# A fused group-norm and 4-bit grouped convolution: a new prologue, a new statistics chain and end, and one store for two images

## The chip, the cores and the metric

The kernel runs on one core of a Trainium2 chip. The time is the device time of one execution in microseconds (us). Before the change it is 264.53 us, the median of 3 runs (264.43 to 264.54).

## What is computed

`x` has 32 images of 512 channels and 28x28 pixels in float32. Each image is normalised over 32 groups of 16 channels, giving `v`. Cut to what matters:

```python
v   = (x - mean_group) / sqrt(var_group + 1e-5)
xa  = round(clip((v[next conv group] - lA) / (uA - lA), 0, 1) * 15) / 15
wq  = 2 * (round(clip((weight - lW) / (uW - lW), 0, 1) * 15) / 15 - 0.5)
y   = einsum('bgihw,goi->bgohw', xa, wq.reshape(4, 128, 128))
y   = relu(batch_norm(y, gamma, beta, running_mean, running_var))
out = x + y + v
```

The kernel writes `max(conv, floor) + (x * y_scale + y_bias)`, where `floor` and the batch norm's offset are folded into per-channel constants. Input and output are 51.4 MB each.

## The kernel before

**Tiling.** 128 channels lie on the partitions, so an image is four tiles of 128x784, one per convolution group g; output group o of g is (g + 3) mod 4. `images` is a ring of 12 images in SBUF. An image is loaded into its place, read by every stage, turned in place into the output, and stored from there. Statistics and coefficients are made for a pair of images (u = n // 2), so that 16 chains serve 32 images.

**The steps of one image.** (1) Statistics: VectorE takes groups 0 and 1 (groups 0 to 2 for the first six images) with `bn_stats` (L435, `half_stats`), and at the pair's second image `sum_stats` (L443); ScalarE takes the other groups with a sum (L218) and a sum of squares (L224). (2) The chain of the pair: TensorE averages the means over norm groups (`average_means`, L533, L534, L536), ScalarE copies them (`copy_mean`, L232), GpSimd makes deviations (`deviations`, L350 to L357), TensorE averages their squares (`average_deviations`, L542), ScalarE takes the root (`deviation`, L238, L239), VectorE its reciprocal (`rough_rstd`, L468), and GpSimd a Newton step and the four coefficients (`coefficients`, L370 to L379, nine small instructions). (3) Quantise: three tiles on ScalarE (L251), one on GpSimd (L397), then VectorE caps all four at once into bf16 (`cap`, L450). (4) TensorE multiplies each tile by the weights in three bf16 parts (`multiply`, L552, 6 matmuls a tile, three PSUM sets, so tile k waits for `finish` of tile k - 3). (5) GpSimd scales and shifts the image in place (`affine`, L388), and VectorE adds the two (`finish`, L458).

**Order.** Every engine has an order written out by hand, in slots. In slot n VectorE does finish(n, 0), finish(n, 1), cap(n + 1), finish(n, 2), a half statistic, finish(n, 3), and three half statistics of image n + 6 (`AHEAD`); in odd slots `rough_rstd` stands before finish(n, 3). GpSimd does the four `affine` of image n + 1 and the tile of `quantise(n + 2)`, with `deviations` in even slots and `coefficients` at the end of odd ones. In a pair of slots ScalarE does statistics of image n + 6 with `copy_mean` inside, six quantises, `deviation`, and statistics of image n + 7. TensorE puts `average_means` ahead of multiply(n + 1, 0) in even slots and `average_deviations` ahead of multiply(n + 1, 3).

**DMA.** SyncE loads (L183); from image 12 on, the load of image n waits for the store of image n - 12. ScalarE stores images 0 to 27 one by one (L244), each behind a wait for that image's last `finish`; it does so at two places of its pair of slots. SyncE stores images 28 to 30 (L187) and image 31 in four pieces (L196).

**Prologue.** Image 0 is loaded in four pieces, then the weights, then images 1 to 11. GpSimd quantises the weights (L336 to L341) before it turns to the first deviations; the four limits reach all 128 partitions through a broadcast DMA (L204).

Of the kernel before, what the change touches and what calls it, by code (L numbers as in the profile page):

```python
# [5 lines left out]
ALU = mybir.AluOpType  # L6
ACT = mybir.ActivationFunctionType
AXIS = mybir.AxisListType
F32 = mybir.dt.float32
# [12 lines left out]
AHEAD = 6  # L22
ACT_STORES = 28
# [5 lines left out]
def fused_norm_quantised_conv(nc, x, weight, limits, channel_params, out):  # L29
# [14 lines left out]
    def stats_on_dve(u):  # L44
        return 3 if u < AHEAD // 2 else 2


    def quant_on_act(n):
        return 2 if n == 0 else 3

# [18 lines left out]
    with ExitStack() as ctx:  # L69
# [20 lines left out]
        half_var = sb("half_var", [P, 2, G], F32)  # L90
        std = sb("std", [P, 2, G], F32)
        rough = sb("rough", [P, 2, G], F32)
        newt = sb("newt", [P, 3, 2, G], F32)
        three_halves = sb("three_halves", [P, 2, G], F32)
        minus_half = sb("minus_half", [P, G], F32)
        rstd = sb("rstd", [P, 2, G], F32)
        mean_rstd = sb("mean_rstd", [P, 2, G], F32)
        q_scale = sb("q_scale", [P, 2, 2, G], F32)
        q_bias = sb("q_bias", [P, 2, 2, G], F32)
        y_scale = sb("y_scale", [P, 2, 2, G], F32)  # L100
        y_bias = sb("y_bias", [P, 2, 2, G], F32)
# [6 lines left out]
        cols = sb("cols", [P, 4, G], F32)  # L108
        bounds = sb("bounds", [P, 4], F32)
        w_rng = sb("w_rng", [P, 2], F32)  # L110
        a_rng = sb("a_rng", [P, 5], F32)
        bn = sb("bn", [P, 5, G], F32)
        bias_bn = sb("bias_bn", [P, G], F32)
# [14 lines left out]
        first_loaded = [sem(f"first_loaded{g}") for g in range(G)]  # L128
        x_loaded = [sem(f"x_loaded{j}") for j in range(RING)]
        stored = [sem(f"stored{j}") for j in range(RING)]  # L130
# [31 lines left out]
        y_ready = sem("y_ready")  # L162
# [4 lines left out]
        def wait_image(engine, n, g):  # L167
            if n == 0:
                engine.wait_ge(first_loaded[g], DMA)
            else:  # L170
                engine.wait_ge(x_loaded[n % RING], DMA * (n // RING + (1 if n % RING else 0)))

        @block.sync
        def _(sync):
            for g in (0, G - 1, 1, 2):
                sync.dma_start(images[:, 0, g], x_v[0][:, g]).then_inc(first_loaded[g], DMA)
            sync.dma_start(w_raw[:], weight.rearrange("(g o) i -> o g i", o=P)).then_inc(weights_in, DMA)

            def load(n):
                j = n % RING  # L180
                if n >= RING:
                    sync.wait_ge(stored[j], DMA * (n // RING))
                sync.dma_start(images[:, j], x_v[n]).then_inc(x_loaded[j], DMA)  # L183
# [5 lines left out]
            for n in range(1, B):  # L189
                load(n)  # L190
            for n in range(ACT_STORES, B - 1):
                store(n)
            for g in range(G):
                o = output_group(g)
                sync.wait_ge(final, G * (B - 1) + g + 1)
                sync.dma_start(out_v[B - 1][:, o], images[:, (B - 1) % RING, o]).then_inc(stored[(B - 1) % RING], DMA)  # L196
            for j in range(RING):
                stores = len(range(j, B, RING)) + (G - 1 if j == (B - 1) % RING else 0)
                sync.wait_ge(stored[j], DMA * stores)

        @block.scalar
        def _(act):
            act.dma_start(rows[:], channel_params.rearrange("k (g p) -> (k g) p", p=P)).then_inc(rows_in, DMA)
            act.dma_start(bounds[:], limits.to_broadcast([P, 4])).then_inc(limits_in, DMA)  # L204
# [3 lines left out]
            nc.scalar.activation(cols[:], cols_ps[:, 0:4 * G], ACT.Identity).then_inc(cols_done, 1)  # L208
# [32 lines left out]
            def store(n):  # L241
                if 0 <= n < ACT_STORES:
                    act.wait_ge(final, G * n + G)
                    act.dma_start(out_v[n], images[:, n % RING]).then_inc(stored[n % RING], DMA)  # L244

            def quantise(n, g):
                u, j = n // 2, n % 2
                act.wait_ge(coef_done, u + 1)
                if n >= 2:
                    act.wait_ge(capped, n - 1)  # L250
                nc.scalar.activation(levels[:, n % 2, g], images[:, n % RING, g], ACT.Relu,  # L251
                                     bias=q_bias[:, u % 2, j, g:g + 1],
                                     scale=q_scale[:, u % 2, j, g:g + 1]).then_inc(q_act, 1)
# [15 lines left out]
            copy_mean(1)  # L269
            image_stats(4)  # L270
            deviation(1)
            for g in range(quant_on_act(1)):
                quantise(1, g)
            image_stats(5)

            for n in range(0, B - 2, 2):
                u, m = n // 2 + 2, n + AHEAD
                if m < B:
                    take_sum(m, 2)
                    take_sum(m, 3)  # L280
# [12 lines left out]
                store(n)  # L293
                if m + 1 < B:
                    image_stats(m + 1)

            for n in range(B - 3, ACT_STORES):
                store(n)

        @block.gpsimd  # L300
        def _(pool):
# [9 lines left out]
            nc.gpsimd.memset(three_halves[:], 1.5)  # L311
            nc.gpsimd.memset(minus_half[:], -0.5)
# [19 lines left out]
            nc.gpsimd.tensor_tensor(bias_bn[:], cols[:, 1], bn[:, 4], ALU.subtract)  # L332

            pool.wait_ge(ranges_done, 1)
            pool.wait_ge(weights_in, DMA)
# [267 lines left out]
```

## Time and profile before

| | |
|---|---|
| median of 3 runs | 264.53 us |
| the profiled execution: its time, its span | 266.27 us, 264.5 us |
| busy share of the span: VectorE, GpSimd, ScalarE, TensorE | 89%, 89%, 77%, 70% |
| bytes moved, mean rate | 103.28 MB, 390 GB/s |
| share of the chain that ended last on GpSimd | 72% |

The span is that of one profiled execution on the core; the time of that execution has some 1.8 us around it. A busy share is an average over the prologue, 26 like slots, and an end without loads and statistics. The rate of the DMA engines is the second resource that everything shares.

### The profile page before, as it was taken

What the parts mean: (1) busy time and instruction counts of PE and PEld (TensorE: products, weight loads), DVE (VectorE), ACT (ScalarE), POOL (GpSimd) and SP (SyncE); (2) the same over time, 40 slices, a digit from 0 to 9 for tenths busy, and PEclk for the clock granted to TensorE, in tenths of its full rate; (3) what the DMA queues carried; (4) which work ended last, traced back from release to release, by engine and by line L of the source; (5) the groups of instructions that cost most, each with busy time, mean ns of one, the idle gap of its engine ahead of it and who ended that gap; (6) DMA issues with size and microseconds to landing.
All of it is one profiled execution on the core that took longest, in us unless ns stands there. A gap on an engine that the chain in (4) does not pass through costs nothing.

```text
span 264.5 us, 4055 instructions
## 1 busy us (share of the span) xinstructions
PE 184.9 (70%) x997; PEld 103.7 (39%) x997; DVE 235.7 (89%) x359; ACT 204.7 (77%) x378; POOL 235.4 (89%) x383
## 2 busy tenths in 40 slices
PE   0024498677779797788868678978777797775870
PEld 0023455344445453444425244445443454432330
DVE  1476989999999999999999999999999999795790
ACT  2344699999898999899998989898989696908000
POOL 6395689999999999999999999999999999999940
PEclk9999999999979899988999997979999869999597
DMA  5999999999999999999999999999999999999468
GB/s 154 402 410 410 410 406 408 414 397 331 417 416 416 408 417 417 415 417 417 414 413 417 416 417 417 415 415 417 415 417 417 417 412 402 393 397 375 178 243 327
DMA packets 34614, 103.28 MB, mean 390 GB/s; under 512 B 1296, under 2 KB 1824, under 8 KB 34592
## 3 DMA queue, kind: packets, MB, share of 16 engines
q1 hardware_dynamic: 19632, 58.07, 55.7%
q10 hardware_dynamic: 14960, 44.97, 42.6%
q8 instruction: 8, 0.13, 0.2%
q14 instruction: 14, 0.11, 0.1%
HBM read 51.65 MB, written 51.38 MB: 389 GB/s over the span
## 4 chain that ended last, share of the span: by engine, by line
POOL 72%; issue 9%; DVE 5%; PE 5%; DMA 3%; ACT 2%; ACTq 1%; POOLq 1%; DVEq 0%; SPq 0%
POOL images L388 50%; POOL levels L397 7%; DMA images<-in_x 3%; PE prod L552 2%; POOL q_bias L378 2%; DVE stats L435 2%; PE var_ps L542 1%; ACT levels L251 1%; POOL newt L371 1%; DVE images L458 1%; POOL newt L372 1%; POOL rstd L373 1%; POOL dev L350 1%; POOL mean_rstd L374 1%; POOL dev L353 1%
## 5 line engine op out<-in xcount | busy, mean ns | idle before, releaser
L552 PE MATMUL prod<-codes,w_t 128*128 128x392 bf16 x768 | 156.2, 354 | 35.2 <-DVE images L458 21.0
L388 POOL TENSOR_SCALAR images<-images,y_scale,y_bias 128x784 f32<-128x784 f32 x128 | 147.7, 1167 | 0.0
L458 DVE SCALAR_TENSOR_TENSOR images<-prod,floor,images 128x784 f32<-128x784 f32 x128 | 126.9, 1016 | 3.0 <-PE prod L552 2.0
L552 PEld LDWEIGHTS prod<-codes,w_t 128*128 128x128 bf16 x768 | 73.7, 105 | 109.2 <-issue 54.6
L251 ACT ACTIVATE levels<-images,q_bias,q_scale 128x784 int16<-128x784 f32 x95 | 90.3, 1029 | 9.5 <-POOL y_bias L379 9.1
L435 DVE BATCH_NORM_STATS2 stats<-images 128x6 f32<-128x392 f32 x140 | 70.7, 551 | 11.0 <-DMA images<-in_x 11.0
L218 ACT ACTIVATE unused<-images 128x784 bf16<-128x784 f32 x58 | 49.2, 851 | 11.8 <-DMA images<-in_x 10.9
L224 ACT ACTIVATE unused<-images,sums 128x784 bf16<-128x784 f32 x58 | 54.6, 944 | 3.0 <-issue 2.8
L450 DVE TENSOR_SCALAR codes<-levels 128x3136 bf16<-128x3136 int16 x32 | 42.2, 1319 | 4.3 <-POOL levels L397 4.2
L397 POOL TENSOR_SCALAR levels<-images,q_scale,q_bias 128x784 int16<-128x784 f32 x33 | 32.9, 998 | 0.1
L542 PE MATMUL var_ps<-dev,avg 128*128 128x8 f32 x128 | 18.5, 271 | 13.6 <-POOL dev L357 13.6
L542 PEld LDWEIGHTS var_ps<-dev,avg 128*128 128x128 f32 x128 | 17.2, 208 | 18.9 <-POOL dev L357 18.8
L533 PE MATMUL mean_ps<-sums,avg 128*128 128x4 f32 (+1 forms) x32 | 5.3, 235 | 19.2 <-DVE sums L443 19.2
L533 PEld LDWEIGHTS mean_ps<-sums,avg 128*128 128x128 f32 x32 | 6.3, 214 | 20.8 <-DVE sums L443 19.8
L224 ACT ACTIVATION_READ_ACCUMULATOR unused<-images,sums 128x1 f32 x58 | 11.2, 193 | 0.0
L218 ACT ACTIVATION_READ_ACCUMULATOR unused<-images 128x1 f32 x58 | 11.2, 192 | 0.0
L232 ACT ACTIVATE gmean<-mean_ps 128x8 f32<-128x8 f32 x16 | 2.8, 174 | 10.5 <-PE mean_ps L534 10.5
L536 PE MATMUL var_ps<-sums,avg_n 128*128 128x8 f32 x32 | 6.5, 276 | 0.0
L534 PE MATMUL mean_ps<-sums,avg_one 128*128 128x4 f32 (+1 forms) x32 | 6.4, 271 | 0.0
L238 ACT ACTIVATE half_var<-var_ps,eps 128x8 f32<-128x8 f32 x16 | 4.0, 253 | 3.0 <-PE var_ps L542 3.0
L370 POOL TENSOR_TENSOR newt<-rough 128x8 f32<-128x8 f32 x16 | 3.2, 201 | 3.5 <-DVE rough L468 3.5
L336 POOL TENSOR_SCALAR w_rest<-w_raw,bounds,w_rng 128x512 f32<-128x512 f32 x1 | 2.1, 2087 | 4.4 <-DVE a_rng L478 4.4
(60 smaller groups left out, 84.9 us busy)
## 6 DMA issues: line engine op xcount, KB each, us to landing
images<-in_x SPq DMA_DIRECT2D x31, 1568.0 KB, 13.2
out<-images ACTq DMA_DIRECT2D x28, 1568.0 KB, 15.5
out<-images SPq DMA_DIRECT2D x3, 1568.0 KB, 5.5
images<-in_x SPq DMA_DIRECT2D x4, 392.0 KB, 6.1
out<-images SPq DMA_DIRECT2D x4, 392.0 KB, 5.5
w_raw<-in_weight SPq DMA_DIRECT2D x1, 256.0 KB, 7.6
rows<-in_channel_params ACTq DMA_DIRECT2D x1, 8.0 KB, 2.3
bounds<-in_limits ACTq DMA_DIRECT2D x1, 2.0 KB, 6.2
```

What stands on the lines that cost most here:

```text
L218: nc.scalar.activation(unused[:, g % 2], images[:, n % RING, g], ACT.Identity, scale=1.0 / HW, accum_out=sums[:, u % 2, 0, j, g:g + 1]).th ...
L224: nc.scalar.activation(unused[:, g % 2], images[:, n % RING, g], ACT.Square, scale=-1.0, bias=sums[:, u % 2, 0, j, g:g + 1], accum_out=sum ...
L251: nc.scalar.activation(levels[:, n % 2, g], images[:, n % RING, g], ACT.Relu, bias=q_bias[:, u % 2, j, g:g + 1], scale=q_scale[:, u % 2, j ...
L388: nc.gpsimd.tensor_scalar(here, here, y_scale[:, u % 2, j, o:o + 1], y_bias[:, u % 2, j, o:o + 1], ALU.mult, ALU.add).then_inc(y_ready, 1)
L397: nc.gpsimd.tensor_scalar(levels[:, n % 2, g], images[:, n % RING, g], q_scale[:, u % 2, j, g:g + 1], q_bias[:, u % 2, j, g:g + 1], ALU.mu ...
L435: nc.vector.bn_stats(two, images[:, n % RING, g, h * HALF:(h + 1) * HALF]).then_inc(bn_done, 1)
L450: nc.vector.tensor_scalar(codes[:, n % 2], levels[:, n % 2], 0.0, TOP, ALU.max, ALU.min).then_inc(capped, 1)
L458: nc.vector.scalar_tensor_tensor(out=two, in0=prod[:, k % SETS, :, 0:HALF], scalar=floor[:, o:o + 1], in1=two, op0=ALU.max, op1=ALU.add).t ...
L533: nc.tensor.matmul(mean[:, :, 0:k], avg[:], sums[:, par, 0, :, 0:k], start=True, stop=True)
L536: nc.tensor.matmul(var_ps[:, 0:2 * G], avg_n[:], sums[:, par, 1], start=True, stop=False)
L542: done = nc.tensor.matmul(var, avg[:], dev2[:, :, :, s], start=False, stop=(s == SUBSETS - 1))
L552: done = nc.tensor.matmul(prod[:, k % SETS, h, 0:HALF], w_t[:, part, output_group(g)], codes[:, n % 2, g, h * HALF:(h + 1) * HALF], start= ...
```

## The change

- **Prologue.** Images 0 and 1 are loaded in four pieces each. VectorE, not GpSimd, quantises the weights. The limits come as one row of 16 bytes, and TensorE spreads them with a one-row matmul into `cols`. TensorE turns the weights before the first averages. Multiply(0, 0) goes ahead of the means of pair 1.
- **Chain.** `AHEAD` is 5, and VectorE takes three groups for the first four images only. `average_means`, `copy_mean` (behind the first of three quantises), `deviations` (behind the second affine) and `deviation` (behind an image's statistics) all stand in an odd slot; `rough_rstd` stands behind finish(n, 0) and `coefficients` behind affine(n + 1, 0) of the next, even slot. `coefficients` has seven instructions, of which the last two make all four coefficients.
- **End.** For the last four images ScalarE does two of the four `affine`.
- **Stores.** ScalarE issues one DMA for two images in even slots, behind that slot's statistics and ahead of its quantises, for images 0 to 29. There is one `stored` semaphore per pair of ring places, so a load of image 12 or later waits for the store of both. SyncE stores image 30, and image 31 in four pieces.

```diff
-AHEAD = 6
-ACT_STORES = 28
+AHEAD = 5
+SINGLE = 2
+HELPED = 4
+ACT_STORES = 30
 SETS = 3
...
-        return 3 if u < AHEAD // 2 else 2
+        return 3 if u < 2 else 2
 
 
     def quant_on_act(n):
         return 2 if n == 0 else 3
+
+
+    def affine_on_act(n):
+        return 2 if n >= B - HELPED else 0
+
...
-            for g in (0, G - 1, 1, 2):
-                sync.dma_start(images[:, 0, g], x_v[0][:, g]).then_inc(first_loaded[g], DMA)
-            sync.dma_start(w_raw[:], weight.rearrange("(g o) i -> o g i", o=P)).then_inc(weights_in, DMA)
+            for n in range(SINGLE):
+                for g in (0, G - 1, 1, 2):
+                    sync.dma_start(images[:, n, g], x_v[n][:, g]).then_inc(first_loaded[n][g], DMA)
+                if n == 0:
+                    sync.dma_start(w_raw[:], weight.rearrange("(g o) i -> o g i", o=P)).then_inc(weights_in, DMA)
 
             def load(n):
                 j = n % RING
                 if n >= RING:
-                    sync.wait_ge(stored[j], DMA * (n // RING))
+                    sync.wait_ge(stored[j // 2], DMA * (n // RING))
                 sync.dma_start(images[:, j], x_v[n]).then_inc(x_loaded[j], DMA)
 
             def store(n):
                 sync.wait_ge(final, G * n + G)
-                sync.dma_start(out_v[n], images[:, n % RING]).then_inc(stored[n % RING], DMA)
...
+                sync.dma_start(out_v[n], images[:, n % RING]).then_inc(stored[n % RING // 2], DMA)
+
+            for n in range(SINGLE, B):
                 load(n)
...
-            act.dma_start(bounds[:], limits.to_broadcast([P, 4])).then_inc(limits_in, DMA)
+            act.dma_start(limit_row[:], limits).then_inc(limits_in, DMA)
...
-                if 0 <= n < ACT_STORES:
-                    act.wait_ge(final, G * n + G)
-                    act.dma_start(out_v[n], images[:, n % RING]).then_inc(stored[n % RING], DMA)
+            def store_pair(u):
+                act.wait_ge(final, 2 * G * (u + 1))
+                k = u % (RING // 2)
+                act.dma_start(out_v[2 * u:2 * u + 2].rearrange("j p g f -> p j g f"),
+                              images[:, 2 * k:2 * k + 2]).then_inc(stored[k], DMA)
...
+            def affine(n, g):
+                u, j, o = n // 2, n % 2, output_group(g)
+                act.wait_ge(q_act, q_act_until(n - 1) + o + 1)
+                here = images[:, n % RING, o]
+                nc.scalar.activation(here, here, ACT.Identity, bias=coef[:, u % 2, 1, 1, G * j + o:G * j + o + 1],
+                                     scale=coef[:, u % 2, 0, 1, G * j + o:G * j + o + 1]).then_inc(y_act, 1)
...
-            copy_mean(1)
-            image_stats(4)
-            deviation(1)
-            for g in range(quant_on_act(1)):
-                quantise(1, g)
-            image_stats(5)
-
-            for n in range(0, B - 2, 2):
-                u, m = n // 2 + 2, n + AHEAD
-                if m < B:
-                    take_sum(m, 2)
-                    take_sum(m, 3)
-                    take_squares(m, 2)
-                if u < PAIRS:
-                    copy_mean(u)
-                store(n - 1)
-                if m < B:
-                    take_squares(m, 3)
-                for g in range(quant_on_act(n + 2)):
-                    quantise(n + 2, g)
-                for g in range(quant_on_act(n + 3)):
-                    quantise(n + 3, g)
-                if u < PAIRS:
-                    deviation(u)
-                store(n)
-                if m + 1 < B:
-                    image_stats(m + 1)
-
-            for n in range(B - 3, ACT_STORES):
-                store(n)
+
+            for n in range(-1, B - 1):
+                m = n + AHEAD
+                if n % 2:
+                    u = (n + 3) // 2
+                    for g in range(quant_on_act(n + 2) if n + 2 < B else 0):
+                        quantise(n + 2, g)
+                        if g == 0 and u < PAIRS:
+                            copy_mean(u)
+                    if m < B:
+                        image_stats(m)
+                    if u < PAIRS:
+                        deviation(u)
+                    for g in range(G - affine_on_act(n + 1), G):
+                        affine(n + 1, g)
+                else:
+                    for g in range(G - affine_on_act(n + 1), G):
+                        affine(n + 1, g)
+                    if m < B:
+                        image_stats(m)
+                    if n:
+                        store_pair(n // 2 - 1)
+                    for g in range(quant_on_act(n + 2) if n + 2 < B else 0):
+                        quantise(n + 2, g)
...
-            pool.wait_ge(ranges_done, 1)
-            pool.wait_ge(weights_in, DMA)
-            chained(nc.gpsimd.tensor_scalar(w_rest[:], w_raw[:], bounds[:, 0:1], w_rng[:, 1:2], ALU.subtract, ALU.mult))
...
-            for g in range(G):
-                scaled = nc.gpsimd.tensor_scalar(w_raw[:, g], w_rest[:, g], bn[:, 3, g:g + 1], None, ALU.mult)
-            scaled.then_inc(w_scaled, 1)
...
-                linked(u, 4, nc.gpsimd.tensor_tensor(rstd[:], newt[:, 2], rough[:], ALU.mult))
-                nc.gpsimd.tensor_tensor(mean_rstd[:], gmean[:, par], rstd[:], ALU.mult).then_inc(coef_step, 1)
-                nc.gpsimd.tensor_scalar(q_scale[:, par], rstd[:], a_rng[:, 2:3], None, ALU.mult)
-                nc.gpsimd.tensor_scalar(y_scale[:, par], rstd[:], 1.0, None, ALU.add)
-                pool.wait_ge(coef_step, LINKS * u + 5)
-                nc.gpsimd.tensor_scalar(q_bias[:, par], mean_rstd[:], a_rng[:, 4:5], a_rng[:, 3:4], ALU.mult, ALU.add)
-                nc.gpsimd.tensor_tensor(y_bias[:, par], bias_bn[:].unsqueeze(1).to_broadcast([P, 2, G]), mean_rstd[:],
-                                        ALU.subtract).then_inc(coef_done, 1)
+                linked(u, 4, nc.gpsimd.tensor_tensor(norm[:, 0], newt[:, 2], rough_, ALU.mult))
+                linked(u, 5, nc.gpsimd.tensor_tensor(norm[:, 1], gmean[:, par].rearrange("p j g -> p (j g)"), norm[:, 0],
+                                                     ALU.mult))
+                linked(u, 6, nc.gpsimd.tensor_tensor(scaled[:], norm[:].unsqueeze(2).to_broadcast([P, 2, 2, 2 * G]),
+                                                     coef_mul[:].unsqueeze(3).to_broadcast([P, 2, 2, 2 * G]), ALU.mult))
+                nc.gpsimd.tensor_tensor(coef[:, par], scaled[:], coef_add[:], ALU.add).then_inc(coef_done, 1)
...
             coefficients(0)
             quantise(0)
-            deviations(1)
-            affine(0, 0)
-            affine(0, 1)
-            coefficients(1)
-            affine(0, 2)
-            affine(0, 3)
-            quantise(1)
-            for n in range(B - 1):
-                for g in range(G):
+            for n in range(-1, B - 1):
+                mine = G - affine_on_act(n + 1)
+                for g in range(mine):
                     affine(n + 1, g)
-                if n % 2 == 0 and n // 2 + 2 < PAIRS:
-                    deviations(n // 2 + 2)
+                    if n % 2 and g == 1 and (n + 3) // 2 < PAIRS:
+                        deviations((n + 3) // 2)
+                    if n % 2 == 0 and g == 0 and (n + 2) // 2 < PAIRS:
+                        coefficients((n + 2) // 2)
                 if n + 2 < B:
                     quantise(n + 2)
-                if n % 2 == 1 and (n + 3) // 2 < PAIRS:
-                    coefficients((n + 3) // 2)
...
+            group_stats(0, 0)
+            dve.wait_ge(cols_done, 1)
...
+            group_stats(0, 1)
+            group_stats(0, 2)
+
+            dve.wait_ge(weights_in, DMA)
+            chained(nc.vector.tensor_scalar(w_rest[:], w_raw[:], bounds[:, 0:1], w_rng[:, 1:2], ALU.subtract, ALU.mult))
...
+            dve.wait_ge(floor_done, 1)
+            for g in range(G):
+                done = nc.vector.tensor_scalar(w_raw[:, g], w_rest[:, g], bn[:, 3, g:g + 1], None, ALU.mult)
+            done.then_inc(w_scaled, 1)
 
             image_stats(1)
             sum_stats(0)
-            image_stats(2)
-            rough_rstd(0)
-
             dve.wait_ge(w_turned, 1)
...
+            group_stats(2, 0)
+            group_stats(2, 1)
+            rough_rstd(0)
+            group_stats(2, 2)
             image_stats(3)
             sum_stats(1)
             cap(0)
             image_stats(4)
-            rough_rstd(1)
-            image_stats(5)
-            sum_stats(2)
-            dve.wait_ge(floor_done, 1)
 
             for n in range(B):
                 m = n + AHEAD
                 finish(n, 0)
+                if n % 2 == 0 and (n + 2) // 2 < PAIRS:
+                    rough_rstd((n + 2) // 2)
                 finish(n, 1)
                 if n + 1 < B:
                     cap(n + 1)
                 finish(n, 2)
                 if m < B:
                     half_stats(m, 0, 0)
-                if n % 2 == 1 and (n + 3) // 2 < PAIRS:
-                    rough_rstd((n + 3) // 2)
                 finish(n, 3)
                 if m < B:
...
+            pe.wait_ge(limits_in, DMA)
+            nc.tensor.matmul(cols_ps[:, 4 * G:5 * G], one_row[:], limit_row[:], start=True,
+                             stop=True).then_inc(cols_turned, 1)
...
-            average_means(0)
-            average_deviations(0)
             pe.wait_ge(w_scaled, 1)
-            pe.wait_ge(cols_done, 1)
             for g in range(G):
                 turned = nc.tensor.transpose(prep_ps[:, g], w_raw[:, g], ident[:])
             turned.then_inc(w_turned, 1)
-            average_means(1)
-            average_deviations(1)
+            average_means(0)
+            average_deviations(0)
             pe.wait_ge(w_ready, 1)
-            for g in range(G):
-                multiply(0, g)
-
-            for n in range(B - 1):
-                chain = n % 2 == 0 and n // 2 + 2 < PAIRS
+
+            for n in range(-1, B - 1):
+                chain = n % 2 == 1 and (n + 3) // 2 < PAIRS
+                if chain and n > 0:
+                    average_means((n + 3) // 2)
+                multiply(n + 1, 0)
+                if chain and n < 0:
+                    average_means((n + 3) // 2)
                 if chain:
-                    average_means(n // 2 + 2)
-                multiply(n + 1, 0)
+                    average_deviations((n + 3) // 2)
                 multiply(n + 1, 1)
                 multiply(n + 1, 2)
-                if chain:
-                    average_deviations(n // 2 + 2)
                 multiply(n + 1, 3)
```

## Rows read from the trace of the kernel before

**Rows 1.** The page: busy time and share by engine; the DMA's total.
```profile
PE 184.9 (70%) x997; PEld 103.7 (39%) x997; DVE 235.7 (89%) x359; ACT 204.7 (77%) x378; POOL 235.4 (89%) x383
...
DMA packets 34614, 103.28 MB, mean 390 GB/s; under 512 B 1296, under 2 KB 1824, under 8 KB 34592
```

**Rows 2.** The chain that ended last, two pieces: start us, us, engine, tile, line, count.
```profile
181.73 4.63 POOL images L388 x4
...
195.93 4.64 POOL images L388 x4
```

**Rows 3.** Stretches: us, busy time by engine, granted clock, DMA share, GB/s.
```profile
54.50:66.50 12.00, 9.13 (x54) 4.75 (x53) 11.97 (x20) 11.65 (x23) 11.77 (x16) 1.00 1.00 360
70.00:200.00 130.00, 103.20 (x571) 56.30 (x570) 129.69 (x194) 122.63 (x230) 126.48 (x201) 0.93 1.03 416
...
225.00:240.00 15.00, 12.23 (x74) 6.65 (x74) 12.31 (x14) 6.91 (x10) 14.61 (x23) 1.00 1.01 393
```

**Rows 4.** ScalarE's first store, by line and in its stretch: issue and landing.
```profile
L244 ACTq DMA_DIRECT2D out<-images x1: 402/402/402, 46.1 to 46.1; - x1
...
DMA to landing us min/median/max: 11.9/11.9/11.9
```

**Rows 5.** Timeline, VectorE: start us, us, engine, line, operation, count, idle time before.
```profile
202.33 1.70 DVE L450 TENSOR_SCALAR codes<-levels 128x3136 bf16<-128x3136 int16 x1
...
208.06 1.97 DVE L458 SCALAR_TENSOR_TENSOR images<-prod,floor,images 128x784 f32<-128x784 f32 x2
209.94 1.01 DVE L450 TENSOR_SCALAR codes<-levels 128x3136 bf16<-128x3136 int16 x1
...
214.64 1.01 DVE L458 SCALAR_TENSOR_TENSOR images<-prod,floor,images 128x784 f32<-128x784 f32 x1
```

**Rows 6.** Timeline, from finish(26, 0) to the copy of the means.
```profile
222.26 1.96 DVE L458 SCALAR_TENSOR_TENSOR images<-prod,floor,images 128x784 f32<-128x784 f32 x2
...
223.43 1.16 PE L552 MATMUL prod<-codes,w_t 128*128 128x392 bf16 x6 [1.34 <-DVE images L458]
...
224.96 0.18 ACT L232 ACTIVATE gmean<-mean_ps 128x8 f32<-128x8 f32 x1 [2.19 <-PE mean_ps L534]
```

**Rows 7.** Timeline, ScalarE: two statistics in a row, six quantises, the root.
```profile
48.32 0.85 ACT L218 ACTIVATE unused<-images 128x784 bf16<-128x784 f32 x1
...
52.05 0.86 ACT L218 ACTIVATE unused<-images 128x784 bf16<-128x784 f32 x1
...
213.23 5.69 ACT L251 ACTIVATE levels<-images,q_bias,q_scale 128x784 int16<-128x784 f32 x6
...
218.82 0.25 ACT L238 ACTIVATE half_var<-var_ps,eps 128x8 f32<-128x8 f32 x1
218.97 0.25 ACT L239 ACTIVATE std<-var_ps,eps 128x8 f32<-128x8 f32 x1
```

**Rows 8.** Timeline, GpSimd: first and last of the nine instructions of coefficients.
```profile
207.80 0.20 POOL L370 TENSOR_TENSOR newt<-rough 128x8 f32<-128x8 f32 x1
...
209.92 0.20 POOL L379 TENSOR_TENSOR y_bias<-bias_bn,mean_rstd 128x8 f32<-128x8 f32 x1
```

**Rows 9.** Timeline, prologue: weights, deviations, first quantise, VectorE's slot 1.
```profile
17.82 2.35 POOL L341 TENSOR_SCALAR w_raw<-w_rest,bn 128x128 f32<-128x128 f32 x4
...
20.14 0.23 POOL L350 TENSOR_TENSOR dev<-stats,gmean 128x24 f32<-128x24 f32 x1
...
26.52 1.97 ACT L251 ACTIVATE levels<-images,q_bias,q_scale 128x784 int16<-128x784 f32 x2 [1.37 <-POOL y_bias L379]
...
45.11 1.95 DVE L458 SCALAR_TENSOR_TENSOR images<-prod,floor,images 128x784 f32<-128x784 f32 x2
```

**Rows 10.** Timeline, the end: finishes of images 26 and 27, then the last six.
```profile
225.06 3.85 DVE L458 SCALAR_TENSOR_TENSOR images<-prod,floor,images 128x784 f32<-128x784 f32 x4
...
252.44 5.73 DVE L458 SCALAR_TENSOR_TENSOR images<-prod,floor,images 128x784 f32<-128x784 f32 x6
```

**Rows 11.** The page's DMA issues: operation, count, KB each, us to landing.
```profile
out<-images SPq DMA_DIRECT2D x3, 1568.0 KB, 5.5
```

More of the change, by code:

```diff
@@ L44, in stats_on_dve, with y_pool_until, y_act_until @@
     def stats_on_dve(u):
-        return 3 if u < AHEAD // 2 else 2
+        return 3 if u < 2 else 2
     def quant_on_act(n):
         return 2 if n == 0 else 3
+    def affine_on_act(n):
+        return 2 if n >= B - HELPED else 0
+    def y_pool_until(n):
+        return sum(G - affine_on_act(i) for i in range(n + 1))
+    def y_act_until(n):
+        return sum(affine_on_act(i) for i in range(n + 1))
     def q_act_until(n):
@@ L89, in fused_norm_quantised_conv @@
         dev2 = sb("dev2", [P, 2, G, SUBSETS], F32)
-        half_var = sb("half_var", [P, 2, G], F32)
+        half_var = sb("half_var", [P, 2 * G], F32)
         std = sb("std", [P, 2, G], F32)
         rough = sb("rough", [P, 2, G], F32)
-        newt = sb("newt", [P, 3, 2, G], F32)
-        three_halves = sb("three_halves", [P, 2, G], F32)
+        newt = sb("newt", [P, 3, 2 * G], F32)
+        three_halves = sb("three_halves", [P, 2 * G], F32)
         minus_half = sb("minus_half", [P, G], F32)
[L96 to L101, printed above, removed]
+        norm = sb("norm", [P, 2, 2 * G], F32)
+        scaled = sb("scaled", [P, 2, 2, 2 * G], F32)
+        coef = sb("coef", [P, 2, 2, 2, 2 * G], F32)
+        coef_mul = sb("coef_mul", [P, 2, 2], F32)
+        coef_add = sb("coef_add", [P, 2, 2, 2 * G], F32)
         w_raw = sb("w_raw", [P, G, P], F32)
@@ L107, in fused_norm_quantised_conv @@
         rows = sb("rows", [4 * G, P], F32)
-        cols = sb("cols", [P, 4, G], F32)
-        bounds = sb("bounds", [P, 4], F32)
+        limit_row = sb("limit_row", [1, 4], F32)
+        one_row = sb("one_row", [1, P], F32)
+        cols = sb("cols", [P, 5, G], F32)
+        bounds = cols[:, 4]
         w_rng = sb("w_rng", [P, 2], F32)
-        a_rng = sb("a_rng", [P, 5], F32)
+        a_rng = sb("a_rng", [P, 2], F32)
         bn = sb("bn", [P, 5, G], F32)
-        bias_bn = sb("bias_bn", [P, G], F32)
         floor = sb("floor", [P, G], F32)
@@ L126, in fused_norm_quantised_conv @@
         cols_ps = prod[:, 1, 0]
-        first_loaded = [sem(f"first_loaded{g}") for g in range(G)]
+        first_loaded = [[sem(f"first_loaded{n}_{g}") for g in range(G)] for n in range(SINGLE)]
         x_loaded = [sem(f"x_loaded{j}") for j in range(RING)]
-        stored = [sem(f"stored{j}") for j in range(RING)]
+        stored = [sem(f"stored{j}") for j in range(RING // 2)]
         rows_in = sem("rows_in")
@@ L161, in fused_norm_quantised_conv @@
         multiplied = sem("multiplied")
-        y_ready = sem("y_ready")
+        y_pool = sem("y_pool")
+        y_act = sem("y_act")
         final = sem("final")
@@ L195, in _ @@
                 sync.wait_ge(final, G * (B - 1) + g + 1)
[L196 to L199, printed above, removed]
+                sync.dma_start(out_v[B - 1][:, o], images[:, (B - 1) % RING, o]).then_inc(stored[(B - 1) % RING // 2], DMA)
+            for k in range(RING // 2):
+                stores = len(range(2 * k, ACT_STORES, RING)) + (1 + G if k == (B - 1) % RING // 2 else 0)
+                sync.wait_ge(stored[k], DMA * stores)
         @block.scalar
@@ L387, in affine @@
                 here = images[:, n % RING, o]
-                nc.gpsimd.tensor_scalar(here, here, y_scale[:, u % 2, j, o:o + 1], y_bias[:, u % 2, j, o:o + 1],
-                                        ALU.mult, ALU.add).then_inc(y_ready, 1)
+                nc.gpsimd.tensor_scalar(here, here, coef[:, u % 2, 0, 1, G * j + o:G * j + o + 1],
+                                        coef[:, u % 2, 1, 1, G * j + o:G * j + o + 1], ALU.mult,
+                                        ALU.add).then_inc(y_pool, 1)
             def quantise(n):
@@ L468, in rough_rstd, with group_stats @@
                 nc.vector.reciprocal(rough[:], std[:]).then_inc(rough_done, 1)
-            image_stats(0)
-            dve.wait_ge(limits_in, DMA)
+            def group_stats(n, g):
+                half_stats(n, g, 0)
+                half_stats(n, g, 1)
+            group_stats(0, 0)
+            dve.wait_ge(cols_done, 1)
             nc.vector.tensor_tensor(w_rng[:, 0:1], bounds[:, 1:2], bounds[:, 0:1], ALU.subtract)
```

58 lines of the change are left out of this document (36 added, 22 removed).

## The prediction

> **What bounds the kernel now.** I read the page first: two engines are busy 89% of the span, and 103.28 MB move at a mean of 390 GB/s [rows 1]. The chain that ended last then says which engine sets the pace. One set of four `affine` starts at 181.73 and the set two slots on at 195.93, so a pair of images costs 14.2 us, and GpSimd fills all of it [rows 2]. The table of stretches adds the DMA's side: 416 GB/s from 70 to 200 us, in which VectorE is busy 129.7 of 130 us too [rows 3]. A pair of images is four transfers of 1.606 MB, 6.42 MB or 15.4 us at 416 GB/s, more than the 14.2 us of compute. The kernel lives on the twelve images it loaded ahead, and the two limits lie within 8% of each other. Whatever lengthens compute above 15.4 us a pair, or leaves the DMA idle early, is paid in full. All bytes at 416 GB/s take 248.3 us.
>
> **Prologue: gain 3.1 us at slot 1.** GpSimd ends the weights at 17.82 + 2.35 = 20.17, and only then makes the deviations, at 20.14 by its overlapping row [rows 9]. On VectorE the same five steps of 512 columns cost about 3 us, since a 784-column finish takes 0.98 (1.97 for two) [rows 5]. Deviations then wait for statistics and come 1.4 to 3.3 us earlier (the smaller value if image 1 lands as before, the larger if the short broadcast DMA no longer disturbs the start); with two fewer small instructions the first quantise moves from 26.52 [rows 9] to about 22 to 24, and I take 23.2. From there: cap at + 3.1 (VectorE still has statistics of image 3), six cold matmuls 1.9, means 1.0, two quantises 1.9, one image's statistics 3.7, root 0.5, reciprocal, and then the rest of slot 0, 6.2. Slot 1 starts at 23.2 + 18.8 = 42.0, against 45.11 [rows 9]. Bounds: 40.5 and 44. The cover is gone here: VectorE waits in slot 0 from finish(0, 0) to the reciprocal, some 6 us.
>
> **Chain: loss 13.8 us.** This is the term that decides. Let O be the start of an odd slot on VectorE. Finish(n, 0) lets TensorE make tile 3, and the means stand right behind it. In slot 26 of the kernel before, which has the same order, the slot starts at 222.26 and the means are copied at 224.96, O + 2.70 [rows 6]. In the new order ScalarE then has, in line: two quantises at 5.69 / 6 = 0.95 each, one image's statistics, 52.05 - 48.32 = 3.73, and the root, 218.97 + 0.25 - 218.82 = 0.40 with 0.06 to VectorE [rows 7]. The root is there at O + 2.70 + 0.15 + 1.90 + 3.73 + 0.46 = O + 8.95. VectorE wants it behind finish(n, 0) of the even slot. Its odd slot without reciprocal is one of 6.58 us (214.64 - 208.06) if the cap takes 1.01, and 7.3 if it takes 1.70 [rows 5], so it asks at O + 7.6 to 8.3 and waits 0.7 to 1.4 us. Behind the reciprocal follow 5.6 us (6.58 less one finish) and 0.24 for the sums; the next odd slot starts at O + 8.95 + 0.1 + 5.84 = O + 14.9, or 15.6 with the long cap. GpSimd waits with it: coefficients stand behind one affine. They cost 209.92 + 0.20 - 207.80 = 2.3 before [rows 8], and about 2.1 with seven instructions, so GpSimd needs 14.0, below the loop. I take 15.05 us a pair (the cap falls beside small GpSimd work, where 1.01 is nearer). Before, the reciprocal stood most of a slot later and this wait was covered. From slot 1 to slot 27 there are 13 pairs: 42.0 + 13 x 15.05 = 237.7; with 14.9 and 15.6 it is 235.7 and 244.8. Before, slot 27 starts at 225.06 + 3.85 / 2 = 227.0 [rows 10]; 13 pairs of 14.2 from 45.11 would give 229.7, and the 2.7 less are the statistics that end one slot earlier with `AHEAD` 6. So the chain and `AHEAD` 5 together cost 13 x 0.85 + 2.7 = 13.8 us. `AHEAD` 5 removes no work; it gives loads one slot more, which the ring's pairing takes back.
>
> **Stores in the middle: no further term, but no slack.** The first store is issued at 46.1 and lands 11.9 us later [rows 4], which frees place 0. In the new order ScalarE issues the pair behind image 7's statistics in slot 2, at about 54.5, when the twelve loads have just ended; the DMA idles some 5 us, and two of about 2 us follow while loads wait for a whole pair to land. The old dip is 360 against 416 GB/s over 12 us, 1.6 us [rows 3]. So 9 us of DMA time are lost where 1.6 were. At 15.05 us a pair the last loads land about 2 us before they are asked for, so this stays hidden behind the chain; it is the limit if the chain is faster. The rows show a 1.606 MB store taking 11.9 us beside loads and 5.5 alone [rows 4, 11], so I let both directions share equally. The Trainium skill, DMA: Bandwidth & Descriptors, section on queues, rings and completion order, says that each DMA engine goes round robin between its rows packet by packet; by that the shared pair takes 15.4 us each way, as I have it. Were stores served first, loads would come later by up to 7.7 us and the sum would be about 6 us higher.
>
> **End: GpSimd's relief is given back by the last pair store, gain 0.5 us.** Eight `affine` leave GpSimd (8 x 1.16 = 9.3 us by four in 4.64 [rows 2]), which would be worth at most that. But ScalarE gets them. From O of slot 27: the root at + 6.0 (no statistics left), two affines each of images 28 and 29 (3.8), store of 26 and 27, three quantises each of images 30 and 31 (5.7), two affines each of 30 and 31 (3.8), and only then the store of images 28 and 29: O + 19.3, although both are finished at about + 16. Behind it lie four images, 6.42 MB; at the 393 GB/s of a stretch that is nearly all stores [rows 3] they take 16.3 us, and 1.4 us of fixed time (5.5 less 1.606 MB / 393 [rows 11]). That ends at O + 37.0. Compute alone ends sooner: 5 slots of 5.1 us, then 264.5 - 258.2 = 6.3 us as before [rows 10], O + 31.8. Before, image 28 was stored on its own, ahead of it, and the end took 264.5 - 227.0 = 37.5. The sum is 264.5 - 3.1 + 13.8 - 0.5 = 274.7; I forecast **275.0 us**. The profiled span before is 264.5 and the median 264.53, so nothing is to be added. The case's own bounds are 235.7 + 34 = 270 and 244.8 + 37 = 282.
>
> **Rivals.** *The DMA decides* (chance 0.18): the root comes in time, because ScalarE's order has more slack than I see, and compute runs at 14.1 us. Then 248.3 us of bytes, 4 for the start (my share of the 264.5 - 248.3 = 16.2 us that the DMA loses now, of which 1.6 are the dip and some 10 the end), 9 of early idle, 2.2 for 41 us of stores alone at 393, and 1.2 at the end give 264.7, and 266 with gaps between stores at the end. For it: ScalarE is busy only 77% [rows 1]. Against: the chain above is in line, whatever the share. *Faster* (0.10): the chain is covered and the first pair store goes out early, by 50 us, so that the early idle stays at 2 us; then the earlier slot 1 and the relief of GpSimd both count, and the DMA ends at 264.7 - 7 = 258 to 260. It decides if the root is ready by O + 7.6. Beside it stands a rule: the same page of the Trainium skill, section rules for kernel authors, wants large DMAs, and the section on the anatomy of one DMA puts about 2 us of fixed cost on each. By it 13 fewer stores would be worth up to 26 us, an estimate. The trace speaks against that: 416 GB/s with single stores leaves no such cost bare [rows 3]. *Nothing* (0.04): the prologue's gain and the lost wait cancel, 264.5. *Chain and DMA add up* (0.04): over 281, if both caps take 1.70 us. The forecast has 0.64.
>
> **How the numbers follow.** The predicted time is the first case's. The range goes from 265 (the second case) to 281; outside lie the faster case, part of the one that cancels, and the worst. A measurement of this kernel tells 0.2%, 0.53 us, from no change. Faster by that has 0.10, within it 0.04, slower 0.86.
>
> **What would show it.** Right: VectorE's reciprocal with an idle time of 0.7 to 1.4 us ahead of it, ended by ScalarE's root, in each even slot; `newt` on GpSimd idle ahead by about 1 us; ScalarE's stores 15 us apart, the first at 54 to 55; a stretch near 52 us with the DMA under half; slot 27 at 236 to 240; the last pair store some 3 us behind the finish of image 29. Wrong: reciprocals with no idle time and a period of 14.2; a first pair store before 51; DMA at 416 GB/s from 45 us on. If the period is right and the end is not, the term of the last pair store was mis-sized.

## The result, and the profile after

The changed kernel takes **269.35 us** (median of 4 runs, 268.73 to 271.67) against 264.53 (median of 4 runs, 264.43 to 265.72): a ratio of 1.018, interval 1.0145 to 1.0212. It is slower, as forecast, but the forecast loss was 10.5 us and the measured one is 4.8.

The page of the changed kernel: busy shares, rate in 40 slices, DMA issues.

```profile
PE 183.2 (69%) x999; PEld 105.5 (40%) x999; DVE 229.3 (86%) x363; ACT 213.0 (80%) x394; POOL 211.5 (79%) x340
...
GB/s 236 402 410 412 407 409 409 313 408 244 369 356 276 409 409 415 416 411 417 413 415 417 418 413 417 417 415 417 417 415 418 417 417 411 349 402 389 244 404 321
...
images<-in_x SPq DMA_DIRECT2D x30, 1568.0 KB, 17.5
out<-images ACTq DMA_DIRECT2D x15, 3136.0 KB, 18.8
```

GpSimd fell from 89% [rows 1] to 79%, so the engine that set the pace is relieved, and the kernel is slower all the same. Stretches of the changed kernel (columns as in [rows 3]), then of the kernel before in the first of them:

```profile
50.00:90.00 40.00, 29.35 (x168) 16.50 (x167) 37.75 (x59) 35.69 (x66) 37.06 (x57) 0.96 0.88 327
...
225.00:250.00 25.00, 21.78 (x119) 12.18 (x117) 22.10 (x29) 21.62 (x30) 20.50 (x32) 0.89 0.87 342
...
247.00:249.00 2.00, 2.00 (x12) 1.07 (x13) 2.00 (x3) 2.00 (x3) 1.76 (x2) 1.00 0.06 24
249.00:251.00 2.00, 2.00 (x14) 1.08 (x12) 2.00 (x3) 2.00 (x3) 0.00 (x0) 1.00 0.64 256
```

```profile
50.00:90.00 40.00, 30.91 (x176) 17.04 (x174) 39.90 (x60) 37.83 (x71) 38.82 (x65) 0.96 1.02 398
```

From 50 to 90 us the DMA moves 327 GB/s where it moved 398, which at 416 is 40 x 71 / 416 = 6.8 us of transfer put off; at 247 us it nearly stands still, since image 28 is finished and may not leave before image 29 is (the lines on this stand in the section on the prediction, under the end). The timeline of one odd slot of the changed kernel shows the chain, to be read beside [rows 5 to 7]:

```profile
187.01 1.97 DVE L475 SCALAR_TENSOR_TENSOR images<-prod,floor,images 128x784 f32<-128x784 f32 x2
...
189.72 0.18 ACT L248 ACTIVATE gmean<-mean_ps 128x8 f32<-128x8 f32 x1 [1.44 <-PE mean_ps L567]
189.79 1.97 ACT L268 ACTIVATE levels<-images,coef 128x784 int16<-128x784 f32 x2
...
191.67 0.84 ACT L234 ACTIVATE unused<-images 128x784 bf16<-128x784 f32 x1
...
195.21 0.25 ACT L254 ACTIVATE half_var<-var_ps,eps 128x8 f32<-128x8 f32 x1
195.36 0.25 ACT L255 ACTIVATE std<-var_ps,eps 128x8 f32<-128x8 f32 x1
195.65 0.20 DVE L485 RECIPROCAL rough<-std 128x8 f32<-128x8 f32 x1 [1.06 <-ACT std L255]
...
201.61 1.97 DVE L475 SCALAR_TENSOR_TENSOR images<-prod,floor,images 128x784 f32<-128x784 f32 x2
```

VectorE waits 1.06 us for the root, and a pair takes 201.61 - 187.01 = 14.60 us instead of 14.2 [rows 2]. What was predicted as hidden is visible too: the chain that ended last runs, from 182 us on, through one pair store, the load it releases, and the statistics of that load (start us, us, what):

```profile
182.73 22.14 DMA out<-images
...
205.30 22.69 DMA images<-in_x
...
228.01 0.02 ACT unused L234
```

### The profile page after: what moved, and what is told of

Same layout as the page of the kernel before. It is cut to its first block and busy times, and to the rows that moved or that the text cites. A ratio compares the mean times of both kernels' runs of the same rounds, so it can differ in the third digit from the quotient of the medians.

```text
span 267.0 us, 4013 instructions
## 1 busy us (share of the span) xinstructions
PE 183.2 (69%) x999; PEld 105.5 (40%) x999; DVE 229.3 (86%) x363; ACT 213.0 (80%) x394; POOL 211.5 (79%) x340
## 3 DMA queue, kind: packets, MB, share of 16 engines
HBM read 51.65 MB, written 51.38 MB: 386 GB/s over the span
## 5 line engine op out<-in xcount | busy, mean ns | idle before, releaser
L585 PE MATMUL prod<-codes,w_t 128*128 128x392 bf16 x768 | 154.0, 350 | 54.2 <-DVE codes L464 28.9
L404 POOL TENSOR_SCALAR images<-images,coef 128x784 f32<-128x784 f32 x120 | 128.6, 1081 | 0.2 <-POOL coef L396 0.2
L268 ACT ACTIVATE levels<-images,coef 128x784 int16<-128x784 f32 x95 | 91.6, 1030 | 0.0
L464 DVE TENSOR_SCALAR codes<-levels 128x3136 bf16<-128x3136 int16 x32 | 34.1, 1066 | 1.4 <-ACT levels L268 1.1
L414 POOL TENSOR_SCALAR levels<-images,coef 128x784 int16<-128x784 f32 x33 | 33.5, 1016 | 0.1
L575 PEld LDWEIGHTS var_ps<-dev,avg 128*128 128x128 f32 x128 | 19.3, 228 | 10.1 <-POOL dev L372 9.8
L485 DVE RECIPROCAL rough<-std 128x8 f32<-128x8 f32 x16 | 3.2, 202 | 18.6 <-ACT std L255 18.6
L365 POOL TENSOR_TENSOR dev<-stats,gmean 128x16 f32<-128x16 f32 (+1 forms) x16 | 4.9, 304 | 12.8 <-ACT gmean L248 12.7
L391 POOL TENSOR_TENSOR norm<-newt,rough 128x8 f32<-128x8 f32 x16 | 12.6, 788 | 1.3
L276 ACT ACTIVATE images<-images,coef 128x784 f32<-128x784 f32 x8 | 7.7, 1032 | 0.0
## 6 DMA issues: line engine op xcount, KB each, us to landing
out<-images ACTq DMA_DIRECT2D x15, 3136.0 KB, 18.8
```

Source lines behind the costliest of these rows:

```text
L391: linked(u, 4, nc.gpsimd.tensor_tensor(norm[:, 0], newt[:, 2], rough_, ALU.mult))
L404: nc.gpsimd.tensor_scalar(here, here, coef[:, u % 2, 0, 1, G * j + o:G * j + o + 1], coef[:, u % 2, 1, 1, G * j + o:G * j + o + 1], ALU.mu ...
L414: nc.gpsimd.tensor_scalar(levels[:, n % 2, g], images[:, n % RING, g], coef[:, u % 2, 0, 0, G * j + g:G * j + g + 1], coef[:, u % 2, 1, 0, ...
L464: nc.vector.tensor_scalar(codes[:, n % 2], levels[:, n % 2], 0.0, TOP, ALU.max, ALU.min).then_inc(capped, 1)
L575: done = nc.tensor.matmul(var, avg[:], dev2[:, :, :, s], start=False, stop=(s == SUBSETS - 1))
L585: done = nc.tensor.matmul(prod[:, k % SETS, h, 0:HALF], w_t[:, part, output_group(g)], codes[:, n % 2, g, h * HALF:(h + 1) * HALF], start= ...
```

## The experiments

Two theories stood against each other. Theory C: the late root lengthens compute. Theory S: paired stores starve the DMA. Each group of runs was timed beside the kernel before, which took 264.53 us beside the change and 265.15 to 265.31 beside the other runs. Differences to the change in us below are between medians and carry that drift of up to 0.8 us; the ratios do not.

| kernel | median, us | ratio to before (interval) |
|---|---|---|
| the change | 269.35 | 1.018 (1.0145 to 1.0212) |
| single stores | 266.59 | 1.006 (1.0039 to 1.0079) |
| root early | 270.36 | 1.019 (1.0151 to 1.0228) |
| root early, single stores | 261.32 | 0.987 (0.9823 to 0.9907) |
| images 28, 29 single | 268.22 | 1.011 (1.0069 to 1.0149) |
| kernel before with pairs | 277.86 | 1.047 (1.0435 to 1.0496) |
| pair store first | 266.96 | 1.006 (1.0040 to 1.0079) |
| root early, pair first | 267.01 | 1.007 (1.0047 to 1.0092) |
| the same, two DMAs | 262.87 | 0.992 (0.9898 to 0.9939) |
| no help at the end | 271.02 | 1.022 (1.0176 to 1.0260) |
| root early, single, no help | 260.76 | 0.984 (0.9816 to 0.9856) |
| root early, single first | 262.35 | 0.989 (0.9868 to 0.9913) |
| weights on GpSimd | 269.87 | 1.021 (1.0163 to 1.0250) |

**Single stores.**

```diff
                     if u < PAIRS:
                         deviation(u)
+                    store(n - 1)
...
-                    if n:
-                        store_pair(n // 2 - 1)
+                    store(n - 1)
```

> The changed kernel with one store per image again, one in each slot on ScalarE, and one store semaphore per ring place; prologue, chain and end stay. Theory S (the paired stores cost the time: DMA idle near 51, 61 and 80 us while loads wait for a pair, and at 247 to 250 us while the last pair is not yet issued): those four dips in the DMA rate go, no load is waited for at the end, and the time falls by 4 to 5 us from the 269.35 of the changed kernel, to about 265, level with the kernel before. Theory C (the chain costs it: ScalarE's root comes 1.06 us late for VectorE's reciprocal in every pair, 14.60 us a pair): the dips go but the time falls by at most 1.5 us, and the period stays 14.60.

Measured: 2.8 us less than the change (3.2 by the ratios). From 50 to 90 us the rate is 381, the period stays 14.60 (reciprocals at 50.14 and 64.73), and the kernel is still 0.6% slower than before. So stores are part of the loss, by less than theory S said.

**The root early.**

```diff
-                    if m < B:
-                        image_stats(m)
+                    for g in range(stats_on_dve(m // 2), G if m < B else 0):
+                        take_sum(m, g)
                     if u < PAIRS:
                         deviation(u)
+                    for g in range(stats_on_dve(m // 2), G if m < B else 0):
+                        take_squares(m, g)
```

> The changed kernel with ScalarE's root (deviation) moved ahead of the two sums of squares, behind the two sums, in odd slots, 1.9 us earlier; paired stores stay. Theory C: VectorE's 1.06 us wait ahead of each reciprocal goes, the period falls from 14.60 to GpSimd's 14.0 to 14.1, and the time falls by 5 us to about 264. Theory S: the period falls as said, but loads then bind from some 150 us on, since the DMA idles early as before; ScalarE's waits for loads grow by what the chain saved, and the time falls by less than 2 us.

Measured: no gain. The period falls to 13.9 (reciprocals at 131.85 and 145.73, no idle time), then rises to 15.5 (190.79 and 206.28), and ScalarE's waits for loads grow from 9.9 to 18.0 us. Its chain from 134 us on is a loop of transfers:

```profile
134.90 21.97 DMA out<-images
...
157.30 21.40 DMA images<-in_x
...
178.72 0.03 ACT unused L234
...
180.55 22.13 DMA out<-images
```

A pair store frees two places, the load lands, ScalarE makes the statistics, and behind them in its queue stands the store of the pair three on: 180.55 - 134.90 = 45.65 us for three pairs, 15.2 each. Faster compute alone buys nothing. This is what theory S said of this run.

**Both.** The two edits together.

> Both edits together: the root ahead of the squares, and one store per image in each slot. If each theory holds for its own part and the two parts hide each other, the gain is more than the sum of the two alone: period 14.0 to 14.1, no early DMA idle, and 259 to 261 us, faster than the kernel before. If theory S alone is right: no faster than single stores alone, about 265. If theory C alone is right: as with the root alone, about 264.

Measured: 8.0 us less than the change and 3.8 less than the kernel before beside it (265.15), a little above the 259 to 261 expected. One edit alone gave 2.8, the other nothing. So each theory holds for its own part, and the two parts hide each other: each limit alone is enough to keep the kernel slow. Stretches of this kernel:

```profile
50.00:90.00 40.00, 31.76 (x183) 18.12 (x182) 39.73 (x62) 38.76 (x73) 38.51 (x58) 0.96 1.03 402
90.00:200.00 110.00, 83.42 (x486) 47.03 (x485) 109.73 (x167) 105.05 (x197) 105.62 (x161) 0.98 1.03 416
225.00:250.00 25.00, 17.17 (x102) 9.23 (x100) 19.42 (x22) 14.84 (x18) 12.47 (x20) 0.94 1.03 401
```

**The last pair.** `ACT_STORES` is 28, and SyncE stores 28, 29 and 30.

> The changed kernel with images 28 and 29 stored one by one by SyncE instead of as ScalarE's last pair; all other pairs stay. Theory S: the DMA idle of 2.6 us at 247 to 250 us goes, and the time falls by 2 to 3 us, to about 267. Theory C (compute alone sets the end): no change beyond 0.5 us.

Measured: 1.1 us less by the medians, but the intervals touch and the two profiled spans are 267.4 and 267.0. The dip at 247 us is gone; what it was worth stays unresolved, below the 2 to 3 us expected.

**The kernel before, with pairs alone.**

```diff
-                store(n - 1)
+                store_pair(n // 2 - 1)
 ...
-                store(n)
```

> The kernel before with one part of the change alone: ScalarE stores images 0 to 27 as pairs (issued where the odd image's store stood, behind the third statistic of an even slot), and a load of image 12 or later waits for the pair; SyncE stores 28 to 31 as before; prologue, chain and end are the old ones. Theory S: the first store goes out at about 54.7 instead of 46.1, the DMA idles about 9 us between 50 and 85 us as in the changed kernel, and though VectorE and GpSimd keep their 14.2 us a pair, loads bind before the end: 269 to 271 us, 4 to 6 above the kernel before. Theory C: the compute order is untouched, so at most 1 us more.

Measured: 12.6 us slower, two to three times the 4 to 6 that theory S said. With `AHEAD` 6 each load is asked for one slot sooner, so ScalarE waits 31.4 us for loads where the kernel before waits 10.9, and its store stands behind that wait:

```profile
ACT unused L219 <- DMA images<-in_x: 31.4, 7, 5.2
```

That `AHEAD` 5 is what makes the pairs of the changed kernel bearable is argued from this; the changed kernel with `AHEAD` 6 was not run.

**The pair store first.** `store_pair` stands ahead of `image_stats(m)`.

> The changed kernel with ScalarE's pair store ahead of the statistics of its slot instead of behind them; still one DMA for two images. Theory S in the form that the lateness of the issue costs: all pair stores but the last leave 3.6 us earlier, the first at 47.8, the early DMA idle falls from 9 to about 5 us, and the time falls by 2 to 3.5 us to about 266.5. In the form that the size of the pair costs (a place comes free only when both images are out): less than 1 us gained.

> The root ahead of the squares, and the pair store ahead of the slot's statistics. Lateness form of theory S: loads no longer bind as they did with the root alone, and most of the 9 us that separate the root alone from root and single stores come back: 263 to 265 us. Size form: 268 to 270, as with the root alone.

Measured: 2.4 us less than the change without the early root, as the lateness form of theory S said; 3.4 less than the early root alone, which lies between the two forms. With the late root nothing more is to be had: single stores give 266.59 and the pair store first 266.96, and the intervals overlap. With the early root lateness explains 3.4 us, but 5.7 us to single stores are left.

**Two DMAs at the pair's place.** The same wait for both images, then two DMAs, each with its own semaphore.

```diff
-                act.dma_start(out_v[2 * u:2 * u + 2]..., images[:, 2 * k:2 * k + 2]).then_inc(stored[k], DMA)
+                for n in (2 * u, 2 * u + 1):
+                    act.dma_start(out_v[n], images[:, n % RING]).then_inc(stored[n % RING], DMA)
```

> As the run with the root early and the pair store first (267.0), but at the same place, behind the same wait for both images, ScalarE issues two DMAs of one image each with a semaphore per ring place. If the merged DMA itself costs (the first image's place comes free only when both are out), loads are released earlier here and the time falls towards the 261.3 of single stores in every slot, to 263 or less. If the waiting for the second image is what costs, it stays within 1 us of 267.

Measured: 4.1 us less. First stores to landing, merged and then as two:

```profile
L260 ACTq DMA_DIRECT2D out<-images x1: 426/426/426, 46.9 to 46.9; - x1
DMA to landing us min/median/max: 14.0/14.0/14.0
```

```profile
L260 ACTq DMA_DIRECT2D out<-images x2: 426/472/519, 46.8 to 47.2; - x2
DMA to landing us min/median/max: 10.2/11.9/13.7
```

The same bytes leave at the same time, but the first place is free at 57.0 instead of 60.9, and ScalarE's waits for loads fall from 17.2 to 4.7 us. Of the 9.0 us between root early with late pairs (270.36) and with single stores (261.32), 3.4 are lateness, 4.1 come with splitting the DMA and its semaphore, and 1.6 are left, which fit the wait for the second image but were not tested alone. Two DMAs that share one semaphore were not run, so whether the DMA or the semaphore matters is argued: both forms have landed all bytes of the first pair at 60.9, so for this pair the merged transfer is no slower, and only the first place is free later.

**The end and the prologue.** `HELPED` is 0, alone and with root early and single stores; single stores ahead of the statistics or squares of their slots; and the weights quantised on GpSimd again, with TensorE's and VectorE's order around them as before.

> The changed kernel without the end's part: all affines of the last four images on GpSimd again (HELPED 0). GpSimd has 9.3 us more in the last four images, ScalarE 7.7 us less, so the last pair store can leave as soon as image 29 is finished. If the relief of GpSimd counts: 2 to 4 us slower than the changed kernel. If the last store behind ScalarE's affines gives all of it back, as predicted: within 1 us of it.

> Root ahead of the squares, single stores, and no help at the end (all affines on GpSimd). With root and single stores the DMA is busy to the end (400 GB/s from 225 us on) and VectorE has finished at 245.5, 13 us before the end of the span. If the DMA alone then sets the time, GpSimd's 9.3 us more are hidden and the time stays within 1 us of 261.3. If the end of compute still counts, 264 or more.

> Root early and single stores, each store now ahead of its slot's statistics (even slots) or ahead of the squares (odd slots), 2 to 3.6 us earlier. The DMA is the bound by now and has lost some 3 us at the start, 1.4 between 50 and 84 us and little later, so at most 1 us is to be gained: 260.5 to 261.3.

> The changed kernel with one part of the prologue undone: GpSimd quantises the weights again ahead of the first deviations, with TensorE's and VectorE's order around them as before. The first quantise comes 3 to 4 us later and so does slot 1 (44 to 45 instead of 41.1). If the compute of the chain sets the time, the time rises by as much, to 272 to 273. If the loads' release by paired stores sets it, the first pair store is later by the same and the DMA idles 3 us longer, which gives the same; if instead the start is hidden by either, less than 1 us more.

Measured: without help the change is 1.7 us slower by the medians, between the two forecasts, though the intervals overlap. With root early and single stores help is worth nothing (260.76 without, 261.32 with); there the DMA moves 394 and 401 GB/s from 225 to 250 us, so it sets the end. Earlier single stores gain nothing either: 262.35 is above the 260.5 to 261.3 expected, with intervals that overlap. With the weights on GpSimd slot 1 starts at 42.81 instead of 41.06, 1.75 us later and not 3 to 4, and the time is not told apart from the change's.

## Why the prediction was right in direction and wrong in size

The profiled spans give each term of the sum its measured size. The forecast was 264.5 - 3.1 + 13.8 - 0.5 = 274.7. Measured it is 264.5 - 4.05 (slot 1 at 41.06 instead of 45.11) + 8.5 (slot 1 to slot 27 in 190.39 us instead of 181.9) - 1.95 (the end in 35.55 us instead of 37.5) = 267.0. Of the 7.7 us between the two sums, 5.3 are the chain's term, 1.4 the end's and 0.9 the prologue's.

**Prologue.** Right. The first quantise was forecast at 23.2 and starts at 22.46; slot 1 at 42.0 and starts at 41.06; VectorE's wait in slot 0 at 6 us and is 5.44. The six matmuls that the prediction calls cold took 2.12 us against its 1.9, at a granted clock of 1.00 from 26 to 29 us, so the rows don't show that the clock made them slow.

**Chain.** The mechanism is as written, the term is too large, and this is the step that failed: 13.8 us were forecast and 8.5 measured. "I take 15.05 us a pair" measures 14.60 (14.65 on the mean of the 13 pairs, since the last ones wait for loads). The 3.73 us for an image's statistics were read off two starts with a gap of 0.19 us ahead of the second; they take 195.21 - 191.67 = 3.54. The copy to the next quantise takes 0.07 and not 0.15. So the root's reciprocal comes at O + 8.64 and not 8.95. Another 0.15 had been put on top for a long cap. It came in two slots between slot 1 and slot 27, the caps of 1.83 us at 203.50 and 1.71 us at 218.19, both odd slots, where it only shortened VectorE's wait for the root to 0.22 and 0.30 us.

**Stores in the middle.** The forecast idle of 9 us is there (8.5 by the three stretches 50 to 64, 64 to 84 and 84 to 96 us at 284, 351 and 384 GB/s). The first pair store left at 51.38 and not at 54.5. Some of that is the earlier slot 1. But ScalarE's queue also issues a store before the instructions ahead of it have run: the second sum of squares, which stands ahead of it in the program, starts 0.79 us later and ends at 53.11.

```profile
51.38 0.42 ACTq L260 DMA_DIRECT2D out<-images  x1
...
52.17 0.94 ACT L240 ACTIVATE unused<-images,sums 128x784 bf16<-128x784 f32 x1
```

"This stays hidden behind the chain" held only until some 195 us: at 14.60 us a pair the loads fall behind, ScalarE waits 3.15 us for image 31, and the early root showed the two limits to lie on top of each other. A pair's store was also taken at 15.4 us, and it landed in 18.8 at the median, in 22.14 at 182.73. The prediction also gave merging no cost of its own. The rival in which the DMA decides was half right: it took over at the end. The rule for large DMAs that stood beside the rivals counts the other way here: the change issues 15 stores fewer, not 13, and splitting each merged one into two made the kernel 4.1 us faster. The section of the Trainium skill from which the prediction takes 2 us for each DMA is on those that GpSimd issues; all of these leave from ScalarE and SyncE.

**End.** Right in the total within 1.5 us, and wrong in the mechanism. Slot 27 starts at 231.45, not 237.7; the last pair store leaves 17.4 us later, not 19.3; the end comes at 267.0. The prediction had this store wait some 3 us behind ScalarE's affines with both images finished. It did not wait for them. The four finishes of the first line below are two of image 29 and two of image 30; the second starts at 247.8 and takes 1.02 us, so image 29 is finished at 248.8, and the store leaves at 248.84, before the two affines of image 31 that stand ahead of it in the program:

```profile
246.84 3.85 DVE L475 SCALAR_TENSOR_TENSOR images<-prod,floor,images 128x784 f32<-128x784 f32 x4
...
248.84 0.38 ACTq L260 DMA_DIRECT2D out<-images  x1
...
249.19 1.96 ACT L276 ACTIVATE images<-images,coef 128x784 f32<-128x784 f32 x2
```

Without help slot 27 starts at 231.42, image 29 is finished at 250.3 and the store leaves at 250.30. So in the profiled runs the help brought the last pair store forward by 1.5 us, and nothing of it was given back in ScalarE's queue. What that is worth in the time stays unresolved: undoing the help or the last pair changed the time by no more than the intervals.

**The reference.** All times here lie some 1.7 us above their spans, and the profiled execution before (266.27) lay 1.7 above the median. So the two spans differ by 2.5 us and the medians by 4.8; a sum made against one span carries that error.

## What to carry to other kernels

When two resources are within a few per cent of each other, a part that costs nothing alone can cost all of its price once the other is mended: test parts in pairs. With a ring of buffers, the unit of a store is also the unit in which places come free, and a store behind a wait for a load in an in-order queue closes a loop. Take a duration between two starts only if the first work fills all the time between them. The place of a store in a queue of instructions is not the time at which it leaves: compare its issue with the end of the work it waits for.

## What was not expected

Pairing the stores of the old kernel costs 12.6 us although the DMA moves 411 GB/s from 90 to 200 us; one merged store of two images landed in 14.0 us where the first of two separate ones landed in 10.2. When ScalarE issues two stores in a row, the second issue can be slow: in the run with two DMAs it took 1.03 to 5.08 us between 144 and 207 us, against 0.38 to 0.45 for the first; why stays open. The best version found, root early and single stores without help, takes 260.76 us, 1.6% below the kernel before.
